# Semaphore increments moved from trailing drains to the last instruction of each group, in an RWKV-style macaron layer on eight cores

## The reference, cut to what matters

```python
def ffn(x):                     # x is layer-normed; W_r, W_k, W_v are 1024x1024
    x_prev = shift_by_one_token(x)
    xr = mu_r * x + (1.0 - mu_r) * x_prev
    xk = mu_k * x + (1.0 - mu_k) * x_prev
    r = sigmoid(xr @ W_r.T)
    k_act = square(relu(xk @ W_k.T))
    return r * (k_act @ W_v.T)

def attn(x):
    k, v = mix(x, mix_k) @ Wk.T, mix(x, mix_v) @ Wv.T
    r = sigmoid(mix(x, mix_r) @ Wr.T)
    # per head and token t: eu = exp(u + k_t), ek = exp(k_t)
    #   out_t = (sa + eu * v_t) / (sb + max(sum(eu), 1e-6))
    #   sa = ew * sa + ek * v_t;  sb = ew * sb + sum(ek)
    return (r * wkv(k, v)) @ Wo.T

x = x + 0.5 * ffn(layernorm(x))
x = x + attn(layernorm(x))
x = x + 0.5 * ffn(layernorm(x))
```

## Time and profile before

| | |
|---|---|
| median of 3 runs | 3746.83 us (3740.08 to 3841.19) |
| time of the profiled execution | 3742.44 us |
| its span on the slowest core, core 3 | 3740.9 us |
| span of the other cores | 3722.9 to 3740.7 us |
| PE busy | 1812.1 us, 48% of the span |
| PE weight loads | 773.9 us, 21% |
| VectorE (DVE) busy | 1582.1 us, 42% |
| ScalarE (ACT) busy | 771.2 us, 21% |
| mean granted TensorE clock, core 3 | 0.719 of full speed |

### The profile page before, as it was taken

The page is one execution under the profiler, slowest core; times in us unless marked ns, Lnnn a source line. Parts: engine busy times, 40 slices in busy tenths (PEclk is TensorE's granted clock), DMA queues, the critical chain, the costliest instruction groups (busy, mean ns, idle before and its releaser), DMA issues.

```text
span 3740.9 us, 26572 instructions; the slowest of 8 cores (3722.9 to 3740.9 us)
## 1 busy us (share of the span) xinstructions
PE 1812.1 (48%) x7192; PEld 773.9 (21%) x7192; DVE 1582.1 (42%) x3754; ACT 771.2 (21%) x1222; POOL 6.5 (0%) x11
## 2 busy tenths in 40 slices
PE   2454545545455445544454444455454544444544
PEld 0121222222222212222122222122221222221221
DVE  1544444344434444433444444444444444444443
ACT  1222221221212211122222122221222221222221
POOL 0000000000000000000000000000000000000000
PEclk9777766677676766767777777776666777777777
DMA  9000000000000000000000000000000000000000
GB/s 164 12 12 12 1 12 12 12 12 0 12 12 12 12 8 4 12 11 12 12 0 12 12 12 12 12 0 12 12 12 12 1 12 12 12 12 12 1 6 12
DMA packets 18224, 50.07 MB, mean 13 GB/s; under 512 B 2593, under 2 KB 2722, under 8 KB 18082
## 3 DMA queue, kind: packets, MB, share of 16 engines
q0 software_dynamic: 7280, 14.68, 2.6%
q1 hardware_dynamic: 6194, 16.92, 1.4%
q10 hardware_dynamic: 4608, 16.78, 1.1%
HBM read 46.27 MB, written 16.78 MB: 17 GB/s over the span
## 4 chain that ended last, share of the span: by engine, by line
PE 48%; DVE 18%; ACT 12%; issue 9%; DVEq 9%; ACTq 3%; DMA 1%; POOL 0%; POOLq 0%
PE p L368 21%; PE p L370 19%; DVEq L353 5%; PE p L310 4%; PE p L505 2%; PE p L502 2%; DVE s1F L253 2%; ACT junk L246 2%; DVE dbuf L339 2%; ACT ka_fm L423 2%; ACT zfF L321 2%; DVE z_tmF L286 1%; DMA fwvt_s<-fwvt 1%; DVEq L529 1%; DVE numb L523 1%
## 5 line engine op out<-in xcount | busy, mean ns | idle before, releaser
L368 PE MATMUL p<-fwvt_s,ka_fm 128*128 128x512 bf16 x512 | 277.9, 543 | 316.3 <-ACTq L424 316.3
L368 PE MATMUL p<-fwrt_s,xr 128*128 128x512 bf16 x512 | 271.3, 530 | 317.2 <-DVEq L353 317.2
L310 PE MATMUL p<-idb_s,z_tmF 128*128 128x128 bf16 x512 | 64.7, 306 | 631.5 <-DVEq L288 631.5
L370 PE MATMUL p<-fwvt_s,ka_fm 128*128 128x512 bf16 x512 | 273.1, 533 | 0.0
L370 PE MATMUL p<-fwrt_s,xr 128*128 128x512 bf16 x512 | 265.9, 519 | 0.0
L368 PE MATMUL p<-fwkt_s,xk 128*128 128x512 bf16 x512 | 193.8, 379 | 93.4 <-ACTq L390 93.4
L430 DVE TENSOR_TENSOR u_sb<-recbF,p 128x512 f32<-128x512 f32 x64 | 44.0, 687 | 439.0 <-PE p L370 434.5
L368 PE MATMUL p<-wkt_s,xk 128*128 128x512 bf16 x256 | 139.7, 546 | 160.6 <-DVEq L353 160.6
L370 PE MATMUL p<-fwkt_s,xk 128*128 128x512 bf16 x512 | 193.9, 379 | 0.0
L310 PEld LDWEIGHTS p<-idb_s,z_tmF 128*128 128x128 bf16 x512 | 49.5, 137 | 661.0 <-issue 661.0
L246 ACT ACTIVATE junk<-R 128x1024 bf16<-128x1024 f32 x96 | 101.4, 1056 | 387.7 <-DVEq L434 343.0
(11 more groups left out here) (114 smaller groups left out, 3145.1 us busy)
## 6 DMA issues: line engine op xcount, KB each, us to landing
R<-x SPq DMA_DIRECT2D x32, 512.0 KB, 3.3
out<-R ACTq DMA_DIRECT2D x32, 512.0 KB, 2.7
fwrt_s<-fwrt POOLq DMA_DIRECT2D x1, 2048.0 KB, 20.7
fwkt_s<-fwkt POOLq DMA_DIRECT2D x1, 2048.0 KB, 37.8
fwvt_s<-fwvt POOLq DMA_DIRECT2D x1, 2048.0 KB, 49.6
wkt_s<-wkt POOLq DMA_DIRECT2D x1, 2048.0 KB, 62.2
wvt_s<-wvt POOLq DMA_DIRECT2D x1, 2048.0 KB, 73.2
wrt_s<-wrt POOLq DMA_DIRECT2D x1, 2048.0 KB, 85.1
```

The costliest lines, as they stand in the source:

```text
L310: last = t.transpose(p0bank[:, cc * 128:(cc + 1) * 128], src[:, cc * 128:(cc + 1) * 128], idb[:])
L368: t.matmul(pa[:], lhsbuf[:, cc * 128:(cc + 1) * 128], wv[:, cc, 0:512], start=st, stop=sp)
L370: last = t.matmul(pb[:], lhsbuf[:, cc * 128:(cc + 1) * 128], wv[:, cc, 512:1024], start=st, stop=sp)
```

## The change

In 23 groups of VectorE and ScalarE the last line `return v.drain()` or `return s_.drain()` goes, and the instruction ahead of it is returned in its place, so that it carries the semaphore's increment. Drains between two dependent instructions of one group stay, as do those of the prologue. Waits, order, shapes and data are the same. The diff, with hunks of the same form left out:

```diff
-            v.tensor_scalar(L["varb"][:], L["varb"][:], 1e-5, None, ALU.add)
-            return v.drain()
+            return v.tensor_scalar(L["varb"][:], L["varb"][:], 1e-5, None,
+                                   ALU.add)
         emit("v", v12, waits=_w(ev_sq, s1_ev, r_ev), inc="v")
...
-            v.tensor_scalar(z_tm[slot][:], R[:], L["invb"][:],
-                            L["negmib"][:], ALU.mult, ALU.add)
-            return v.drain()
+            return v.tensor_scalar(z_tm[slot][:], R[:], L["invb"][:],
+                                   L["negmib"][:], ALU.mult, ALU.add)
         emit("v", v3, waits=_w(ev_inv, track["zT_" + slot]), inc="v")
...
         def sev(s_):
-            s_.copy(zf3[slayer][:, :, 1:129],
-                    p0[:].rearrange("p (cc t) -> p cc t", cc=8))
-            return s_.drain()
+            return s_.copy(zf3[slayer][:, :, 1:129],
+                           p0[:].rearrange("p (cc t) -> p cc t", cc=8))
...
                 if ti == len(targets) - 1:
                     v.drain()
-                    v.tensor_copy(z3[:, :, 0:1], z3[:, :, 128:129])
-                return v.drain()
+                    last = v.tensor_copy(z3[:, :, 0:1], z3[:, :, 128:129])
+                return last
             war = [track[id(dst)]] if ti > 0 else \
...
         def sesig(s_):
             s_.activation(esig[:, 0:512], p5[:], AF.Exp, scale=-1.0)
-            s_.activation(esig[:, 512:1024], p6[:], AF.Exp, scale=-1.0)
-            return s_.drain()
+            return s_.activation(esig[:, 512:1024], p6[:], AF.Exp,
+                                 scale=-1.0)
...
         def vden(v):
-            v.tensor_scalar(denb[:], esig[:], 1.0, None, ALU.add)
-            return v.drain()
+            return v.tensor_scalar(denb[:], esig[:], 1.0, None, ALU.add)
...
             s_.activation(denb[:], denb[:], AF.Ln)
             s_.drain()
-            s_.activation(recbF[:], denb[:], AF.Exp, scale=-1.0)
-            return s_.drain()
+            return s_.activation(recbF[:], denb[:], AF.Exp, scale=-1.0)
...
         def vka(v):
-            v.tensor_mul(ka_tm[:], krelu[:], krelu[:])
-            return v.drain()
+            return v.tensor_mul(ka_tm[:], krelu[:], krelu[:])
...
             v.drain()
-            v.tensor_add(R[:], R[:], u_sb[:])
-            return v.drain()
+            return v.tensor_add(R[:], R[:], u_sb[:])
...
             v.drain()
             v.tensor_add(numb[:], t2b[:], EKV[:])
+            last = None
             for g in range(4):
-                v.tensor_mul(
+                last = v.tensor_mul(
                     Apv[0:1, 4 * g:4 * (g + 1), :],
                     PG[g][0:1, 0:260].rearrange("p (h c) -> p h c", h=4),
                     bc(ew128[0:1, 4 * g:4 * (g + 1)], 65, parts=1))
-            return v.drain()
+            return last
         emit("v", vepi, waits=[evw], inc="v")
```

More of the change, by code:

```diff
@@ L245, in ssq @@
         def ssq(s_):
-            s_.activation(junk[:], R[:], AF.Square, accum_out=L["s2"][:])
-            return s_.drain()
+            return s_.activation(junk[:], R[:], AF.Square,
+                                 accum_out=L["s2"][:])
         emit("s", ssq, grp="ssq", waits=_w(r_ev, track["v2_" + slot]),
@@ L277, in s2f @@
             s_.drain()
-            s_.activation(L["invb"][:], L["lnvb"][:], AF.Exp, scale=-0.5)
-            return s_.drain()
+            return s_.activation(L["invb"][:], L["lnvb"][:], AF.Exp,
+                                 scale=-0.5)
         emit("s", s2f, grp="s2f", waits=[ev_v2], inc="s")
@@ L408, in srelu @@
             s_.activation(krelu[:, 0:512], p5[:], AF.Relu)
-            s_.activation(krelu[:, 512:1024], p6[:], AF.Relu)
-            return s_.drain()
+            return s_.activation(krelu[:, 512:1024], p6[:], AF.Relu)
         emit("s", srelu, grp="act", waits=[evk], inc="s")
@@ L422, in skev @@
         def skev(s_):
-            s_.copy(ka_fm[:], p0[:])
-            return s_.drain()
+            return s_.copy(ka_fm[:], p0[:])
         emit("s", skev, waits=[evt2], inc="s", grp="kevac")
@@ L454, in s_ek @@
             s_.activation(ek[:, 0:512], p1[:], AF.Exp)
-            s_.activation(ek[:, 512:1024], p2[:], AF.Exp)
-            return s_.drain()
+            return s_.activation(ek[:, 512:1024], p2[:], AF.Exp)
         emit("s", s_ek, grp="act", waits=[evk], inc="s")
@@ L470, in vek @@
             v.drain()
-            v.tensor_mul(ahv, EKVv, bc(utab[:], 65))
-            return v.drain()
+            return v.tensor_mul(ahv, EKVv, bc(utab[:], 65))
         emit("v", vek, waits=[es_, evv], inc="v")
@@ L478, in sesig @@
             s_.activation(esig[:, 0:512], p1[:], AF.Exp, scale=-1.0)
-            s_.activation(esig[:, 512:1024], p2[:], AF.Exp, scale=-1.0)
-            return s_.drain()
+            return s_.activation(esig[:, 512:1024], p2[:], AF.Exp,
+                                 scale=-1.0)
         emit("s", sesig, grp="act", waits=[evr], inc="s")
@@ L491, in sreca @@
             s_.drain()
-            s_.activation(recbA[:], denb[:], AF.Exp, scale=-1.0)
-            return s_.drain()
+            return s_.activation(recbA[:], denb[:], AF.Exp, scale=-1.0)
         emit("s", sreca, grp="rec", waits=[evden], inc="s")
@@ L536, in srec16 @@
             s_.drain()
-            s_.activation(recip16[:], r16ln[:], AF.Exp, scale=-1.0)
-            return s_.drain()
+            return s_.activation(recip16[:], r16ln[:], AF.Exp,
+                                 scale=-1.0)
         emit("s", srec16, grp="rec", waits=[evn], inc="s")
@@ L544, in vepi2 @@
             v.drain()
[L545 to L548, removed]
+            return v.tensor_mul(g2[:].rearrange("p (h d) -> p h d", h=H),
+                                t2v[:, :, 0:64], recbA[:].rearrange(
+                                    "p (h d) -> p h d", h=H))
         emit("v", vepi2, waits=[evr16, evreca], inc="v")
@@ L554, in sgev @@
         def sgev(s_):
-            s_.copy(gfm[:], p0[:])
-            return s_.drain()
+            return s_.copy(gfm[:], p0[:])
         emit("s", sgev, waits=[evt2], inc="s", grp="kevac")
@@ L562, in vro @@
             v.tensor_add(R[:, 0:512], R[:, 0:512], p1[:])
-            v.tensor_add(R[:, 512:1024], R[:, 512:1024], p2[:])
-            return v.drain()
+            return v.tensor_add(R[:, 512:1024], R[:, 512:1024], p2[:])
         emit("v", vro, waits=[evo], inc="v")
```

## The result

The changed kernel takes 3679.4 us (median of 10 runs), the kernel before 3745.6 us in the same series; the ratio is 0.983, with a 95% interval of 0.9815 to 0.9841. The profiled execution took 3679.1 us. The forecast was 3676 us.

The account below looks back on a forecast made before the run. The kernel was taken as a chain of handoffs through PE, ACT and DVE, no engine full. Thirty intervals at 112.63 us save 63 us, the ends 3 more: 3742 - 66 = 3676 us, range 3640 to 3715.

Parts of the forecast that it names:

- The drains' share of the chain: Drains hold 12% of the chain, but the view books working instructions under them; only the tail behind the last is added.
- (a): Handoff to another engine without the trailing drain: 0.09 to 0.10 us instead of 0.13 from L270; 0.02 to 0.03 saved each.
- (b): Next group on the same engine, waits taken earlier: gains 0.29 (L492 to L246), 0.25 (L537 to L423), 0.16 (L563 to L253).
- The third: L563 to L253 on VectorE: still waits for L563's own increment, so falls to 0.10 us, a gain of 0.16.
- (c): TensorE's slow-starting streams: earlier starts bring clock rises a 3.4 us step earlier, making all thirty tile intervals about 112.6 us.
- the plain sum: Rival: the clock averages out and time falls by the fixed 44 us, to 3698 us; chance 22%.
- in one more stream: Among five slow-starting streams per tile, the shorter tile, by about 3.4 us, has the clock's rise a step earlier in one more.
- The fixed sum: Savings of (a) and (b) along one tile's chain: 1.39 us a tile, 44 us over 32 tiles.
- one of two lengths: Tile time, read at L513, is about 116.0 or 112.6 us, some 3.4 us apart, differing by the clock.
- The stated test: Sign against (c): handoffs shrink as said, but L513's intervals do not follow to 112.6 us.

Follow-up runs that it names:

- the handoffs alone: The changed kernel with three drains put back, behind the old L492, L537 and L563: 3731.6 us, ratio 0.997.
- the three places: The kernel before with only the drains behind L492, L537 and L563 removed, where the same engine goes on along the chain: 3704.6 us, ratio 0.990.
- the merged waits: The changed kernel with each group's waits cut to those its engine has not yet seen, one per semaphore: 3536.1 us, ratio 0.945.
- the time put back: The changed kernel with three or one one-column instructions, each with its drain, added in the attention layer norm: 3696.2 us with three, 3685.5 with one.
- one drain less: The kernel before without only the drain of L564, behind the sum into R in attn_d: 3763.2 us, ratio 1.0055.

## Why the prediction was right

The time, 3679 against 3676, and the thirty intervals, 112.65 each against 112.63 forecast, came as worked out. Step by step:

**The drains' share of the chain** was read rightly: DVEq went, DVE took it over, and the span fell by 1.7%.

**(a) Handoffs.** 0.09 us as forecast. Their sum was 0.69; the kernel with the handoffs alone shows 0.82. By the Trainium skill, "Perfetto Trace Analysis", Per-instruction lifecycle, an engine instruction pushes its semaphore update at its reported end. The trace is in line with it: the consumer starts 0.09 us behind the end of L270.

**(b) The same engine.** For two places right (0.32 and 0.25 against 0.29 and 0.25). The third was mis-sized: 0.34, forecast 0.16. The step that failed is "the third must still wait for L563's own increment (r_ev)". The event passed there is rF1 of the next tile, as the main loop's arguments show; only the name r_ev was read. By the Trainium skill, "VectorE: DVE Perf Modes", The DRAIN you can't avoid, chaining without semaphores saves nothing on VectorE. That speaks of the flush in the pipe behind each operation. For the drain instruction the trace shows a saving: L253 starts 0.09 us before L550's end, where it started 0.26 behind L563's.

**(c) The clock.** For short tiles the mechanism is seen: the fwrt stream of F2 had its rise a step earlier (3.2 us low instead of 5.8), and the two streams behind it run low for 5.4 and 4.6 us, forecast 5.4 and 4.5. For long tiles it is seen in F1's fwvt stream (3.2 us low instead of 5.6). All tiles kept the short length, on all eight cores, which no mixture by the plain sum gives. One reading behind it was wrong: that the shorter tile has its rise earlier "in one more stream". The long tile has it later in F1's fwvt stream but earlier in F2's fwrt stream (2.7 us low against 5.8).

The split was off: the forecast gave the clock 22 of 66 us, and it is about 8 of 64. The fixed sum was 1.39 and is 1.7 to 1.8, so its 44 us should have been 56. And the low clock in the WKV matmuls, which the steps of (c) left out, takes 0.26 us a tile more than before; the first fwvt stream runs low for 3.2 and not 3.8 us. The forecast time did not suffer, because all but 3 us of its saving were worked out from the length 112.63 and not from the fixed sum.

In part the hit is luck. The plain-sum rival, with the right fixed sum, would have said 3742 - 56 = 3686, 7 us above what was measured; with the sum that stood there it said 3698. The total is therefore no proof of (c); the equal intervals and the low times of the single streams are. And the steps gave the right length for this kernel alone: for the handoffs, the three places, the merged waits and the time put back the same reasoning missed.

**What the text claimed too widely:** that a tile takes one of two lengths. It holds for the kernel before and for the kernel with one drain less, in the stretches in which its wvt stream runs at full clock. It does not hold for the handoffs alone, the three places or the merged waits, where lengths in between follow each other. The stated test, "if the handoffs shrink as said and the lengths do not follow", would have marked (c) wrong for all of these.

Not settled: what makes one kernel hold a length and another mix them. For the single drain whose removal costs 20 us the trace shows six tiles that stay long where they were short, but not why they do.

## What to carry to other kernels

A trailing drain costs a handoff only 0.02 to 0.03 us, but where the same engine goes on along the chain it costs 0.25 to 0.34, since it also holds back the next group's waits; find those places by the event each group waits for, not by its parameter's name. Repeated waits on semaphores that an engine has already seen cost more (0.42 us ahead of a projection here, 3.8 us a tile) and fall to a few lines of bookkeeping. Where TensorE's streams start at the low clock, judge an edit of under 1% by the pauses it shortens and not by the time alone, because the clock can add or take as much. Before you compare tile lengths, look at a stream that follows another without a pause: if its granted clock is lower than in the other trace (0.81 against 1.00 here), leave that stretch out.

## What the runs showed of the hardware that was not expected

One program ran its tiles at 112.6 and at 116.1 us in one execution on one core, by the granted clock alone (0.74 and 0.69), and all eight cores changed between the two at the same tiles. A kernel with 0.3 us less fixed time a tile was 0.55% slower than its parent. Matmuls in PE's pauses, some 206 a tile, cut the kernel before by 10% (3743 to 3374 us), with a granted clock of 0.99 instead of 0.72. At one place 17 fewer of them cost 56 and 20 us of that, but nothing in the kernel with merged waits.
